# A shared feed-forward taken out of routing: one batch at routing's end, three beside the combination

## What is computed

```python
o = attention(...)                      # (2048, 512)
xf = o + o @ W_out
scores = softmax(xf @ gate_w.T)
topk_w, topk_idx = top_k(scores, 6)
# each expert takes the first 128 tokens that chose it, in order
eo = (silu(gx @ Wg) * (gx @ Wu)) @ down_proj * weight     # per expert
routed = scatter_add(eo)
shared = silu(xf @ shared_gate_w.T) * (xf @ shared_up_w.T) @ shared_down_w.T
return x1 + routed + shared             # x1: the input with its first attention added
```

## Time and profile before

| | |
|---|---|
| three runs | 4120.44, 4127.17, 4131.12 us; median 4127.17 |
| the profiled execution | 4131.14 us, of which 4129.4 from its first to its last instruction (the span) |
| routing, from 3424.6 | 261.5 us |
| experts, from 3686.1 | 356.6 us |
| combination, from 4042.7 | 86.7 us |

### The profile page before, as it was taken

One profiled execution on the slowest core, in us unless ns is written; L12 is line 12 of the kernel. 1 busy time (PEld: TensorE's weight loads), 2 busy tenths in 40 slices (PEclk: granted clock), 3 DMA queues, 4 the chain that ended last, 5 costly groups with the idle time before them and its releaser, 6 DMA issues. The chain is left out here.

```text
span 4129.4 us, 169714 instructions
## 1 busy us (share of the span) xinstructions
PE 3765.6 (91%) x68952; PEld 2476.5 (60%) x68983; DVE 2341.0 (57%) x6671; ACT 1317.8 (32%) x4227; POOL 521.5 (13%) x1107
## 2 busy tenths in 40 slices
PE   7999999999999999998799999878999998969990
PEld 3788888888888888887444444334333334435550
DVE  2555555555555555555477777733666664423336
ACT  0233333333333333333244444422444441111110
POOL 0000000001001000000122222200000002431110
PEclk9999999999999999999999999988999998989995
DMA  4910000000000000001111111021111111229987
GB/s 111 368 41 0 0 0 0 0 0 0 0 0 0 0 0 0 0 0 31 53 55 36 53 36 53 1 84 39 54 53 53 53 55 62 88 80 297 303 269 287
DMA packets 144030, 270.20 MB, mean 65 GB/s; under 512 B 23273, under 2 KB 70517, under 8 KB 140002
## 3 DMA queue, kind: packets, MB, share of 16 engines
q1 hardware_dynamic: 109570, 194.03, 13.9%
q10 hardware_dynamic: 20992, 57.17, 4.8%
q0 software_dynamic: 13408, 18.20, 1.3%
HBM read 148.41 MB, written 89.39 MB: 58 GB/s over the span
## 5 line engine op out<-in xcount | busy, mean ns | idle before, releaser
L310 PE MATMUL gru_pr<-ahead,h 128*4 128x128 f32 x16384 | 558.0, 274 | 14.0 <-DVE h L414 14.0
L310 PE MATMUL gru_pz<-ahead,h 128*4 128x128 f32 x16384 | 542.0, 273 | 4.3 <-issue 4.3
L310 PE MATMUL gru_pn<-ahead,h 128*32 128x128 f32 x16384 | 543.0, 273 | 0.0
L310 PEld LDWEIGHTS gru_pn<-ahead,h 128*32 128x32 f32 x16384 | 459.8, 110 | 1.4
L310 PEld LDWEIGHTS gru_pz<-ahead,h 128*4 128x4 f32 x16384 | 439.1, 87 | 12.1 <-issue 4.9
L310 PEld LDWEIGHTS gru_pr<-ahead,h 128*4 128x4 f32 x16384 | 342.1, 88 | 154.9 <-DVE h L414 25.5
L356 ACT ACTIVATE gru_rn<-gru_pre 128x16 f32<-128x16 f32 x512 | 120.0, 234 | 682.3 <-DVE gru_pre L396 682.3
L394 DVE STREAM_TRANSPOSE gru_tr<-gru_pr 128x128 f32<-128x128 f32 x512 | 162.1, 317 | 291.4 <-PE gru_pr L310 291.4
L273 POOL COPY gru_pick<-ident 128x4 f32 x512 | 95.9, 187 | 1445.2 <-PE gru_pz L301 1439.4
L927 DVE TENSOR_REDUCE da_mx<-da_ps 128x2 f32<-128x1024 f32 (+3 forms) x256 | 201.2, 817 | 131.0 <-PE da_ps L620 131.0
L407 DVE STREAM_TRANSPOSE gru_tz<-gru_pz 128x32 f32<-128x32 f32 (+1 forms) x1024 | 195.2, 229 | 123.0 <-PE gru_pz L310 123.0
(11 more groups left out here) (295 smaller groups left out, 5591.1 us busy)
## 6 DMA issues: line engine op xcount, KB each, us to landing
ahead<-in_L_ffn_gate_up_proj SPq DMA_DIRECT2D x64, 768.0 KB, 6.9
yk<-gru_zeros SPq DMA_DIRECT2D x6, 4096.0 KB, 34.8
ex_wd<-in_L_ffn_down_proj ACTq DMA_DIRECT2D x64, 384.0 KB, 6.1
xg<-gru_zeros SPq DMA_DIRECT2D x4, 4224.0 KB, 31.1
ex_xg<-xg ACTq DMA_DIRECT2D x64, 264.0 KB, 5.8
ahead<-wide SPq DMA_DIRECT2D x15, 1024.0 KB, 4.7
ahead<-xnT SPq DMA_DIRECT2D x15, 1024.0 KB, 4.5
co_got<-yk SPq DMA_DIRECT2D x8, 1536.0 KB, 8.2
```

The lines of the kernel that those rows point to most:

```text
L310: last = nc.tensor.matmul(rows(j), of(c), whh[:, c, g, j, :], start=(c == 0 and start), stop=(c == KD - 1))
```

## The change

In routing the four batches become a pipeline. TensorE starts with the projection as soon as the diagonals are added, and reads the attention output where it lies (`t.oT`) and no longer by way of `ob`; `yT` takes its place there and is kept for all four batches. The projection's fourth tile of a batch comes after the placement of the batch before. ScalarE makes all copies of y and yT. `yb` has three buffers, `slot` and `base` one for each batch. The shared weights are transposed after the last batch's scores and copied by ScalarE; their raw forms are loaded into space of the fourth expert's weights and of `ahead`, so that the load of these expert weights waits for the transposes. After the last placement the shared feed-forward of batch 0 is done. The other three batches' is done in the last stage by TensorE, ScalarE and VectorE, in an order written by hand between the 16 tiles' sums, which now go straight into `x1`. All 16 loads of that stage and 14 of its stores are on SP's queue. The unchanged body of VectorE's choice is left out below, and removed lines are those of the functions above.

```diff
+        NC, R = SI // P, 3
+        wout, stage = t.ro_wout, t.ro_stage
+        suraw = t.ahead[:, 0:NC * D].rearrange("p (c n) -> p c n", c=NC)
+        sdraw = t.ex_wg[:, t.EU - 1, :, :]
+        gwT, yb = sb("gwT", [P, KD, E]), sb("yb", [P, R, TT, XW])
+        above, base = sb("above", [P, 1]), sb("base", [P, B, TT])
...
+            sp.dma_start(sdraw, sd_w.rearrange("(k p) n -> p k n", p=P)).then_inc(raw_in, 16)
+            sp.dma_start(suraw, su_w.rearrange("(c p) n -> p c n", p=P)).then_inc(raw_in, 16)
...
+                if u == t.EU - 1:
+                    sp.wait_ge(shared_psum, 2 * KD + NC)
+                sp.dma_start(t.ex_wg[:, u, :, :], gate_up[u].rearrange("(p k) i -> p k i", p=P)).then_inc(wg_in, 16)
...
+            pe.wait_ge(diag_added, KD)
...
+            def project(b, tts):
+                for tt in tts:
+                    n = b * TT + tt
+                    if n >= 2:
+                        pe.wait_ge(y_copied, n - 1)
+                    for k in range(KD):
+                        last = nc.tensor.matmul(py[:, n % 2, :], t.oT[:, k, b, tt * P:(tt + 1) * P], wout[:, k, :], start=(k == 0), stop=(k == KD - 1))
+                    last.then_inc(y_psum, 1)
...
+            def transpose_y(b):
+                pe.wait_ge(y_copied, b * TT + TT)
...
+                    n = b * KD + k
+                    if n >= 2:
+                        pe.wait_ge(yT_copied, n - 1)
+                    for tt in range(TT):
+                        last = nc.tensor.transpose(pt[:, n % 2, tt * P:(tt + 1) * P], yb[:, b % R, tt, k * P:(k + 1) * P], t.ident[:])
+                    last.then_inc(yT_psum, 1)
...
+            def place(b):
+                if b == 0:
+                    pe.wait_ge(core_set, 2)
+                    pe.wait_ge(before_set, 1)
+                else:
+                    pe.wait_ge(prod_done, b)
+                pe.wait_ge(mask_ready, b + 1)
...
+            project(0, range(TT))
+            transpose_y(0)
+            score(0)
+            for b in range(1, B):
+                project(b, range(0, TT - 1))
+                place(b - 1)
+                project(b, range(TT - 1, TT))
+                transpose_y(b)
+                score(b)
+
+            pe.wait_ge(y_copied, B * TT)
+            pe.wait_ge(raw_in, 32)
+            for n in range(2 * KD + NC):
+                if n >= 2:
+                    pe.wait_ge(shared_copied, n - 1)
+                if n < KD:
+                    for c in range(NC):
+                        last = nc.tensor.transpose(py[:, n % 2, c * P:(c + 1) * P], stage[:, 1 + c, n * P:(n + 1) * P], t.ident[:])
...
+                last.then_inc(shared_psum, 1)
+            place(B - 1)
+
+            def gate_or_up(wT, c, n, done):
...
+                    last = nc.tensor.matmul(bank, wT[:, k, c * P:(c + 1) * P], t.yT[:, k, 0, :], start=(k == 0), stop=(k == KD - 1))
...
+            pe.wait_ge(shared_copied, 2 * KD + NC)
+            for c in range(NC):
+                if c >= 2:
+                    pe.wait_ge(hidden_done, c - 1)
+                gate_or_up(t.sgT, c, 0, gates)
+                gate_or_up(t.suT, c, 1, ups)
+            pe.wait_ge(hidden_done, NC)
+            for tt in range(TT):
+                if tt >= 2:
+                    pe.wait_ge(added, tt - 1)
...
+                    last = nc.tensor.matmul(py[:, tt % 2, :], hT[:, c, tt * P:(tt + 1) * P], t.sdT[:, c, :], start=(c == 0), stop=(c == NC - 1))
+                last.then_inc(down_done, 1)
...
+            for b in range(B):
+                if b >= R:
+                    act.wait_ge(scattered[b - R], ALL)
+                for tt in range(TT):
+                    n = b * TT + tt
+                    act.wait_ge(y_psum, n + 1)
+                    nc.scalar.activation(yb[:, b % R, tt, 0:D], py[:, n % 2, :], ACT.Copy).then_inc(y_copied, 1)
+                for k in range(KD):
+                    n = b * KD + k
+                    act.wait_ge(yT_psum, n + 1)
+                    nc.scalar.activation(t.yT[:, k, b, :], pt[:, n % 2, :], ACT.Copy).then_inc(yT_copied, 1)
...
+            for n in range(2 * KD + NC):
+                act.wait_ge(shared_psum, n + 1)
+                if n < KD:
+                    nc.scalar.activation(t.sgT[:, n, :], py[:, n % 2, 0:SI], ACT.Copy).then_inc(shared_copied, 1)
...
+            for b in range(B):
+                pool.wait_ge(slots_ready, b + 1)
+                pool.sem_inc(tick, 1)
...
+                            out=t.xg_dram, out_offset=bass.IndirectOffsetOnAxis(ap=slot[:, b, tt * K + k:tt * K + k + 1], axis=0),
+                            in_=yb[:, b % R, tt, :], in_offset=None, bounds_check=SLOTS - 1, oob_is_err=False).then_inc(scattered[b], 16)
+            for b in range(B):
+                pool.wait_ge(scattered[b], ALL)
...
+                nc.vector.tensor_tensor(diag, diag, t.ident[:], ALU.add).then_inc(diag_added, 1)
...
+            def choose(b):
+                one = b + 1
+                dve.wait_ge(logits, one)
...
+                dve.wait_ge(carried, b * TT + 1)
+                dve.sem_inc(mask_ready, 1)
+
+                if b >= R:
+                    dve.wait_ge(scattered[b - R], ALL)
+                nc.vector.tensor_copy(yb[:, b % R, :, D], base[:, b, :]).then_inc(noted, 1)
+                nc.vector.tensor_copy(yb[:, b % R, :, D + 1:D + 1 + K], ef[:].rearrange(k24, k=K)).then_inc(noted, 1)
+
+                dve.wait_ge(placed, one)
...
+                dve.wait_ge(noted, b * 2 + 2)
+                nc.vector.tensor_copy(slot[:, b, :], sf[:]).then_inc(slots_ready, 1)
...
+            for b in range(B):
+                choose(b)
+
+            for c in range(NC):
+                dve.wait_ge(silued, c + 1)
+                dve.wait_ge(ups, c + 1)
+                nc.vector.tensor_tensor(hT[:, c, :], sil[:, c % 2, :], (pg if c % 2 == 0 else pt)[:, 1, :], ALU.mult).then_inc(hidden_done, 1)
+            for tt in range(TT):
+                dve.wait_ge(down_done, tt + 1)
+                nc.vector.tensor_tensor(t.x1[:, tt, :], t.x1[:, tt, :], py[:, tt % 2, :], ALU.add).then_inc(added, 1)
...
+def shared_and_combine_stage(nc, t, out):
...
+        def got(n):
+            r = n % R
+            return (t.ahead if r < R // 2 else t.ahead2)[:, (r % 2) * K * D:(r % 2 + 1) * K * D]
+
+        def store(queue, s, n):
+            queue.wait_ge(gathered, n + 1)
+            if n >= TT:
+                queue.wait_ge(added, n - TT + 1)
+            queue.dma_start(out_t[n * P:(n + 1) * P, :], t.x1[:, n, :]).then_inc(stored[s], 16)
 
         @block.sync
         def _(sp):
-            loads_and_stores(sp, 0)
+            def load(n):
+                if n >= R:
+                    sp.wait_ge(gathered, n - R + 1)
+                sp.dma_start(got(n), rows[n]).then_inc(loaded[n % R], 16)
...
+            for n in range(R):
+                load(n)
+            for n in range(R, 2 * R):
+                load(n)
+                store(sp, 0, n - R)
+            for n in range(2 * R, 3 * R):
+                load(n)
+            for n in range(R, 2 * R):
+                store(sp, 0, n)
+            for n in range(3 * R, 4 * R):
+                load(n)
+            for n in range(2 * R, 3 * R):
+                store(sp, 0, n)
+            for n in range(3 * R, 4 * R, 2):
+                store(sp, 0, n)
+            sp.wait_ge(stored[0], 16 * (NTILE - 2))
...
+            for n in range(NC * NB):
+                gate_up(n)
+                if n >= NC and n % NC == 0:
+                    down(n // NC)
+            down(NB)
...
+            for n in range(NC * NB):
+                act.wait_ge(gates, n + 1)
+                if n >= 2:
+                    act.wait_ge(hidden_done, n - 1)
+                nc.scalar.activation(sil[:, n % 2, :], pa[:, 2 * (n % 2), :], ACT.Silu).then_inc(silued, 1)
+            for n in range(3 * R + 1, 4 * R, 2):
+                store(act, 1, n)
+            act.wait_ge(stored[1], 16 * 2)
...
+                        dve.wait_ge(x1_written, n * (K - 1) + k)
+                    nc.vector.scalar_tensor_tensor(x1, got(n)[:, k * D:(k + 1) * D], t.wk[:, b, tt * K + k:tt * K + k + 1], x1,
+                                                   op0=ALU.mult, op1=ALU.add).then_inc(x1_written if k < K - 1 else gathered, 1)
...
+            def hidden(n):
+                b, c = 1 + n // NC, n % NC
+                dve.wait_ge(silued, n + 1)
+                dve.wait_ge(ups, n + 1)
+                if b >= 3:
+                    dve.wait_ge(down_done, (b - 2) * TT)
+                nc.vector.tensor_tensor(hT[:, b % 2, c, :], sil[:, n % 2, :], pa[:, 2 * (n % 2) + 1, :], ALU.mult).then_inc(hidden_done, 1)
...
+            def add_shared(n):
+                dve.wait_ge(down_done, n - TT + 1)
+                dve.wait_ge(gathered, n + 1)
+                nc.vector.tensor_tensor(t.x1[:, n, :], t.x1[:, n, :], pb[:, n % TT, :], ALU.add).then_inc(added, 1)
+
+            gather(0)
+            hidden(0)
```

(77 more changed lines are left out.)

337 lines of the change are left out of this document (112 added, 225 removed).

## The result

| | before | after |
|---|---|---|
| median of four runs each | 4128.62 us | 4064.12 us (4056.02 to 4073.91) |
| ratio | 1 | 0.9848, 95% interval 0.9826 to 0.987 |
| profiled execution | 4131.14, span 4129.4 | 4062.13, span 4059.6 |
| routing starts at | 3424.65 | 3426.76 |
| routing | 261.4 | 176.7 |

The kernel is 64.5 us faster by the medians. Of the 69.8 us between the two spans, routing gives 84.7, the combination takes back 14.5, the experts give 1.7 and the stages before routing take 2.1; the last two were not edited.

What follows compares the result with a forecast made beforehand. Routing was taken as bound by GpSimd's 96 scatters and their waits for slots, the combination by VectorE. Routing -85.9 and combination +13.9 gave -72.0 from 4131.1, 4059.1, or 4055.2 on the median's footing; forecast 4057 us, range 4047 to 4080.

Steps and rivals of the forecast that it cites:

- The start and the first scatter: Routing: projection starts at 3426.2, first scatter at 3467.1, 13.1 us sooner than before.
- the notes moved ahead: Routing, between placement and first scatter: moving the notes ahead saves at most 0.6 us, left out of the sum.
- No wait for slots, the period below 30.7: Routing: a batch costs TensorE 22.7 us, below GpSimd's 30.7 for 24 scatters, so GpSimd never waits again.
- The ring of three y buffers: Routing: ScalarE's first copy of batch 3 waits about 1 us for batch 0's scatters to land; TensorE loses nothing at once.
- The pace: Routing: 95 scatter steps of 1.281 us, 121.7 us from first to last issue, ending at 3588.8; gain 85.9 us.
- the first rival: Routing: scatters and VectorE's choosing collide, costing 4 to 41 us, 12 taken, total 4069; chance 0.11.
- The shared batch costs nothing: Routing's end: shared weights and one feed-forward batch done near 3563, 26 us under the scatters' end, cost nothing.
- The tail of 11.4: Routing's end: 11.4 us pass from the last scatter's issue to the experts' first load.
- The combination: Last stage: 21 added VectorE instructions cost 15.1 us, TensorE runs as long as VectorE; in all +13.9 us.
- The first load: Combination: on one queue the first load lands alone, at 6.1 to 6.5 us instead of 10.0.
- The gaps behind TensorE: Combination: VectorE stands 1.4 us at the third hidden product, and the final tile's addition comes 0.9 behind TensorE.
- The low clock: Combination, rival: TensorE at 1.2 GHz throughout needs 185 us instead of 92.7, +92, total 4149; chance 0.02.

Runs made afterwards that it cites:

- The first experiment: Each batch's fourth tile projected ahead of that batch's placement again, so no pipeline on TensorE, against the changed kernel: routing 175.0 us against 176.7, time 4061.7 us.
- the repeat: The changed kernel, unaltered, run once more beside the last experiment: 4065.5 us, 0.9847 of the kernel before.
- the run of three edits: Changed kernel plus comparison from PSUM, two shared batches in routing with a better combination order, and batch 0 placed right after its scores: 4057.8 us, ratio 0.984.

## Why the prediction was right

The forecast was 4057, in a range from 4047 to 4080; the measured median is 4064.1, at the upper edge of what it called likeliest. Step by step:

- **The start and the first scatter.** Said: the projection 1.6 us into the stage, the first scatter 42.5. Measured 1.0 and 40.9, 1.6 us earlier: 0.6 at the start, 0.2 in the copies of yT, and 0.8 from the scores to the scatter, where 0.4 is what the notes moved ahead save (left out in the sum).
- **No wait for slots, the period below 30.7.** Right: no wait, and a period of 21.9 on TensorE (22.7 said). The first experiment shows what the pipeline gives: without it, GpSimd is fed just in time. Its gain is room under the scatters, and the shorter routing comes without it. The ring of three y buffers held ScalarE for 2.8 us (1 said) and TensorE for 0.2.
- **The pace.** This is the term that was mis-sized: 95 steps of 1.281 were said, 121.7 us; 124.5 us came, 1.310 a step. The 2.8 us are the first rival in small. I had priced it at 12 within 4 to 41 and blamed seven short copies and casts; the runs show that these cost the scatter nothing visible, and that three long comparisons with two SBUF inputs cost nearly all (with one input in PSUM 2.6 us of the stage are gone). The short ones did change: in the kernel before all take 0.17 to 0.18 us, and in the changed one seven of the 21 of batches 1 to 3, while the scatters run, take 0.22 to 0.40. That is VectorE's time, which lies under the scatters; no run tests its cause. -1.6 and +2.8 are the 1.2 by which routing's gain missed the said 85.9.
- **The shared batch costs nothing.** Right: ended at 3561.9 (about 3563 said), 30 us of cover. There was room for a second one, which I had not asked about.
- **The tail of 11.4.** Right, and narrower than I had taken it: it belongs to GpSimd as the last engine.
- **The combination.** +14.5 against +13.9, with VectorE's own work as the main cost, as said. The first load came as said (6.4 in 6.1 to 6.5), the clock rose after 4.6 us, loads never held VectorE. The gaps behind TensorE were 4.5 us where I had counted 1.4 and 0.9. So its two parts, VectorE's work and TensorE's length, were right in kind and the second too small.
- **The low clock** did not come about: 1.00 from 3963.

So the edited stages lost 70.2 us in this profile and 70.8 in the repeat, against 72.0 said. The medians show less, 64.5 and 61.4 (58 to 69 by the repeat's interval). Part of the remainder is that the profiled execution of before, on which the sum was made, lies 2.5 us above its median, and that of after 2.0 below its own. That the total came so close is partly luck: the experts' stage took 355 us in this profile, and the same code took 348 to 363 in the others. In nine of the ten other profiles routing also starts later than before, by 0.5 to 5.6 us, and in one 2.4 earlier; whether the edit has a share in that stays open, since before has only one profile to compare with.

## What to carry to other kernels

Where one engine issues at a fixed pace and the next stage waits for its last issue, count its steps and its start; reordering another engine shortens nothing once that one never waits, it only adds room. Work moved under the issues is free only as far as their end, and an edit elsewhere can use that room up. When two edits draw on the same cover, test them together: here placing the batches early brought the first scatter 2.4 us forward at no cost under one shared batch, and placing batch 0 early lengthened routing by 4.4 under two. Where unedited stages vary by 15 us, judge by the edited stages' own lengths and use totals only with several rounds.

## What the hardware showed

- A VectorE comparison of two SBUF tensors (1.76 us) holds an indirect DMA that GpSimd issues inside it until 0.86 us after its own end; with one input in PSUM the same overlap costs nothing (973 to 1073 ns, 96 times in each of three runs).
- A stage that GpSimd's scatters end hands over 11.4 us after the last issue (3592.13 to 3603.54), one that VectorE ends about 1 us after its last instruction (3563.01 to 3564.05, 3604.76 to 3605.78).
- TensorE's granted clock was 0.50 (1.2 GHz) for the first 4.6 us of the combination, after TensorE had stood for 10.5 us, and from 3458 to 3462 in the run of three edits, after its wait of 7.5 us.
